# Graph network on one core: the one-hot matrices of the edge layers and convolutions made by ScalarE as 1 minus distance instead of compared by VectorE

## What is computed

```python
h = relu(layernorm(x)); x = x + attention(h, src, dst, ...)       # scores, then a weighted sum by dst
h = relu(layernorm(x))
ea = silu(edge_attr @ We + be)
for l in range(4):                                                 # four edge layers
    agg = segment_sum(relu(h[src] + ea), dst)
    h = layernorm(h + mlp(h + agg)) * gamma + beta
x = x + h
h = relu(layernorm(x)); x = x + conv2(conv1(h))                    # two convolutions: segment_sum(h[src] * norm, dst)
h = relu(layernorm(x)); x = x + segment_sum(h[src] @ W, dst) + h @ W_self
```

## Time and profile before

| | |
|---|---|
| device time, median of three runs | 11198.52 us |
| the profiled execution's own time | 11231.99 us |
| its span, first to last instruction | 11230.1 us |
| busy: PE, VectorE, ScalarE, POOL | 6020.5, 3251.3, 1365.6, 6472.3 us |
| mean granted TensorE clock | 0.723 of full speed |
| scores (POOL's gathers) | about 230 to 1525 us of the span |
| weighted sum | 1692 to 2181 us |
| four edge layers | 2215 to 7519 us |
| three convolutions | 7519 to 11230 us |

### The profile page before, as it was taken

The page is one execution under the profiler, slowest core; times in us unless marked ns, Lnnn a source line. Parts: engine busy times, 40 slices in busy tenths (PEclk is TensorE's granted clock), DMA queues, the critical chain, the costliest instruction groups (busy, mean ns, idle before and its releaser), DMA issues. The chain is left out here.

```text
span 11230.1 us, 158248 instructions
## 1 busy us (share of the span) xinstructions
PE 6020.5 (54%) x23911; PEld 4066.9 (36%) x23912; DVE 3251.3 (29%) x7438; ACT 1365.6 (12%) x2091; POOL 6472.3 (58%) x6737
## 2 busy tenths in 40 slices
PE   2556646566665666756666566653344333433344
PEld 1334425433443333433344333332333233333334
DVE  2334467612232122311223122331122112221222
ACT  1112210011221112211122111210000000000000
POOL 2556526466655665556554655546666566656665
PEclk9566669877887788877888778875666555665566
DMA  4777754233322333323332322221111111111111
GB/s 112 206 208 218 219 152 129 86 85 83 84 80 73 86 82 80 82 74 86 82 80 75 83 80 79 77 57 44 46 47 47 44 44 46 44 42 44 45 46 44
DMA packets 982683, 960.66 MB, mean 86 GB/s; under 512 B 442720, under 2 KB 710395, under 8 KB 982137
## 3 DMA queue, kind: packets, MB, share of 16 engines
q0 software_dynamic: 213248, 462.82, 15.6%
q1 hardware_dynamic: 647644, 399.74, 13.3%
q10 hardware_dynamic: 121756, 97.77, 2.7%
HBM read 801.39 MB, written 164.71 MB: 86 GB/s over the span
## 5 line engine op out<-in xcount | busy, mean ns | idle before, releaser
L700 POOL DMA_INDIRECT rows<-node_rows,idx x5488 | 5386.0, 981 | 3647.5 <-SPq L550 1992.6
L1327 DVE SCALAR_TENSOR_TENSOR onehots<-iota_f,win_base,dst_ch 128x512 f32<-128x512 f32 x1969 | 1567.8, 796 | 6664.0 <-remote 3954.8
L832 PE MATMUL ps_seg<-rows,onehots 128*128 x7840 | 1584.2, 368 | 2422.8 <-DVE sums L1348 1089.9
L832 PEld LDWEIGHTS ps_seg<-rows,onehots 128*128 128x128 f32 x7840 | 1383.6, 265 | 2621.6 <-issue 2617.4
L832 PEld LDWEIGHTS ps_seg<-onehots 128*128 128x128 f32 x7840 | 1178.7, 220 | 1744.6 <-issue 962.5
L832 PE MATMUL ps_seg<-onehots 128*128 128x128 f32 x7840 | 1231.4, 307 | 1066.6 <-DVE sums L1348 466.6
L906 PE MATMUL ps_big<-q_res,ident 128*128 (+1 forms) x1968 | 1277.0, 736 | 766.1 <-issue 325.5
L906 PE MATMUL ps_big<-rows,ident 128*128 (+1 forms) x1968 | 1180.7, 686 | 2.1 <-issue 2.1
L700 POOL DMA_INDIRECT sums<-kv_rows,idx x784 | 775.2, 989 | 528.5 <-SPq L550 302.6
L1051 ACT ACTIVATE onehots<-ps_big 128x512 f32<-128x512 f32 x980 | 576.1, 597 | 3251.0 <-remote 1470.5
L906 PEld LDWEIGHTS ps_big<-rows,ident 128*128 128x128 f32 x1968 | 445.1, 227 | 616.3 <-issue 614.0
(11 more groups left out here) (193 smaller groups left out, 2243.4 us busy)
## 6 DMA issues: line engine op xcount, KB each, us to landing
q_res<-gates_by_edge SPq DMA_DIRECT2D x784, 256.0 KB
rows<-node_rows,idx POOLq DMA_INDIRECT x5488
gates_by_edge<-gate ACTq DMA_DIRECT2D x244, 256.0 KB
rows<-dst_padded SPq DMA_DIRECT2D x196, 256.0 KB
value_rows_by_edge<-sums SPq DMA_DIRECT2D x196, 256.0 KB
rows<-value_rows_by_edge SPq DMA_DIRECT2D x196, 256.0 KB, 3.1
idx<-src_padded SPq DMA_DIRECT2D x1568, 2.0 KB
node_rows<-h_res ACTq DMA_DIRECT2D x49, 448.0 KB
```

What stands on the lines that cost most here:

```text
L700: pool.indirect_dma_start(target[:, r, j, :], None, table, bass.IndirectOffsetOnAxis(ap=idx[:, r, j:j + 1], axis=0)).then_inc(rows_landed[ ...
L832: last = nc.tensor.matmul(ps_seg[u % 2][:, 0:width], onehots[:, u, j, :], rhs(j), start=j == 0, stop=j == J - 1)
L1327: V.scalar_tensor_tensor(onehots[:, u, :, :], iota_f[:, :].rearrange("p (a n) -> p a n", a=1).to_broadcast([P, J, P]), win_base[:, ds(w, 1 ...
```

## The change

ScalarE makes the one-hot matrices of the edge layers and convolutions, as max(0, 1 - |node - target|), in six instructions per step: the four offsets of an edge per partition (window's first node minus target, 128x4, function Identity), then for each column the absolute value of `iota_f` plus that offset (128x128, function Abs, the offset as bias), then Relu of 1 minus all four (128x512). It waits for its own result twice in between. VectorE keeps only the additions there; in the weighted sum it still compares. Since ScalarE now goes through the steps of a convolution, its copies and stores of a group hang behind steps of the next iteration, as they did in the edge layers, and the store of a group comes one group later.

```diff
+            def mark_edges(k, s, u, c, w, buffers):
+                n = sum_no(k) * N_ONEHOT - N_ONEHOT
+                nc.scalar.activation(apart[:, u, :], dst_ch[:, ds(c * J, J)], ACT.Identity, bias=win_base[:, ds(w, 1)],
+                                     scale=-1.0).then_inc(apart_ready, 1)
+                wait_alone(act, "act", apart_ready, n + s + 1)
+                for j in range(J):
+                    last = nc.scalar.activation(onehots[:, u, j, :], iota_f[:, :], ACT.Abs, bias=apart[:, u, j:j + 1])
+                last.then_inc(distance_ready, 1)
+                wait_alone(act, "act", distance_ready, n + s + 1)
+                nc.scalar.activation(onehots[:, u, :, :], onehots[:, u, :, :], ACT.Relu, bias=1.0, scale=-1.0)\
+                    .then_inc(onehot_ready, 1)
+
+            def begin_pass(k):
+                wait_alone(act, "act", segsum_ready, sum_no(k) * N_STEP)
+                mark_edges(k, 0, 0, 0, 0, 2)
+
+            def mark_next(k, s, u, row):
+                wait_alone(act, "act", segsum_ready, sum_no(k) * N_STEP + s)
+                mark_edges(k, s + 1, 1 - u, row.get(CHUNK_, CHUNKS - 1, 1), row.get(WIN_, WINDOWS, 1), 2)
...
             with act.Fori(0, LAYERS) as l:
+                begin_pass(l + L1_PASS)
...
                     nc.scalar.activation(msg[:, u, :, 0:D], ps_big[u][:, :].rearrange("p (j d) -> p j d", d=D), ACT.Relu)\
                         .then_inc(msg_ready, 1)
+                    mark_next(l + L1_PASS, s, u, row)
...
-                with engine_loop(act, 0, GROUPS - 1) as g:
-                    copy_group(sum_no(k), g, copies)
-                    store(g)
+                begin_pass(k)
+
+                def convolve(s, u, turn, row):
+                    mark_next(k, s, u, row)
+
+                def conv_store(g):
+                    with act.If(g != 0):
+                        store(one_before(g, GROUPS))
+                each_step(act, "act", convolve, behind={2: lambda g: copy_group(sum_no(k), g, copies), 3: conv_store})
                 copy_group(sum_no(k), GROUPS - 1, copies)
+                store(GROUPS - 2)
                 store(GROUPS - 1)
...
             def add_previous(k, s, u, row, width):
 
+                wait_alone(dve, "dve", segsum_ready, sum_no(k) * N_STEP + s)
                 dve.wait_ge(agg_added, s - 1 + sum_no(k) * N_AGG)
...
                 def edge_layer(s, u, turn, row):
-                    mark_next(k, s, u, row)
                     if not is_first(s):
                         add_previous(k, s, u, row, D)
...
                 def convolve(s, u, turn, row):
-                    mark_next(k, s, u, row)
                     if not is_first(s):
                         add_previous(k, s, u, row, D)
```

More of the change, by code:

```diff
@@ L124, in build_program @@
         part = sb("part", [P, FH])
+        apart = sb("apart", [P, 2, J])
         attr_t = sb("attr_t", [P, 2, P])
@@ L286, in build_program @@
         msg_ready = sem("msg_ready")
+        apart_ready = sem("apart_ready")
+        distance_ready = sem("distance_ready")
         node_in_ready = sem("node_in_ready")
@@ L1336, in begin_pass @@
                     wait_alone(dve, "dve", agg_cleared, sum_no(k) * GROUPS)
-                mark_edges(k, 0, 0, 0, 0)
-            def mark_next(k, s, u, row):
-                dve.wait_ge(segsum_ready, sum_no(k) * N_STEP + s)
-                mark_edges(k, s + 1, 1 - u, row.get(CHUNK_, CHUNKS - 1, 1), row.get(WIN_, WINDOWS, 1))
             def add_previous(k, s, u, row, width):
+                wait_alone(dve, "dve", segsum_ready, sum_no(k) * N_STEP + s)
                 dve.wait_ge(agg_added, s - 1 + sum_no(k) * N_AGG)
@@ L1435, in _ @@
             begin_pass(1)
+            mark_edges(1, 0, 0, 0, 0)
             def mark_ahead(s, u, row, n):
@@ L1446, in attend @@
                 if not is_first(s):
-                    dve.wait_ge(segsum_ready, s)
                     add_previous(1, s, u, row, AGGW)
```

## The result

The changed kernel takes 11532.07 us (median of 4 runs, 11519.61 to 11569.58) against 11203.8 us of the kernel before in the same session (4 runs, 11189.39 to 11227.47): ratio 1.0286, 95% interval 1.0267 to 1.0305. It is 2.9% slower. The forecast was 11390 us with a range of 11060 to 11660.

A forecast was written before the change was run, and what follows sets the result against it. The prediction took POOL's gathers, plus holes where POOL waits for a free slot, as the bound. Gathers -90, convolutions +210 and edge layers +70 gave +190 us on 11198.5, rounded to 11390 us, range 11060 to 11660.

The forecast's parts named there:

- Relief of the gathers, -90 us: POOL's gathers, no longer stretched by compares running beside them, give back half of at most 187 us: -90 us.
- The mark 1.6 us later: ScalarE's six instructions take 2.3 us against 0.75 us of the compare, so the one-hot matrix comes 1.6 us later.
- Convolutions, 70 us each: The later matrix after POOL's holes costs 70 us per convolution, 210 us for three; upper end 585 us.
- One delay per hole: In convolutions, each POOL hole is charged one late mark: 49 holes per 1227 us, 49 x 1.6 = 78 us.
- Edge layers, 17 us each: ScalarE's slower loop costs a fifth of 1.0 us at each of 84 holes: 17 us per layer, 70 for four.
- The prediction's loop of ScalarE: In edge layers, ScalarE's own work takes 3.6 us per step, 1.0 us over TensorE's burst.
- the chain from one sum to the next matrix: In edge layers, the new chain needs 3.5 us and fits in the 4.2 us available.
- Moved work: Convolution copies and clears ahead of marks, 42 us of ScalarE's time, taken as hidden; the later store, 3 us, within rounding.
- the signs of being right: Gathers' mean 960 to 970 ns; POOL's convolution waits about 190 us per 1000; an edge layer within 30 us of 1280.
- The sign against it: A convolution under 1227 us would show the forecast wrong and speak for Rival B.
- Rival A: ScalarE becomes the bound, an edge layer costing 1334 us: +510 us in all, 11710 us; chance 0.17.
- Rival B: Holes end when POOL stops, the later matrix falls into ring slack, POOL keeps 187 us: 11050 us; chance 0.24.

The follow-up runs named there:

- e7: The kernel before with every one-hot compare of the edge layers and convolutions left out, matrices keeping old contents: 9080.56 us, ratio 0.9822.
- e8: The kernel before with VectorE making each matrix in four 128x128 compares with one SBUF tensor each, not one 128x512 with two: 9117.12 us, ratio 0.9865.
- e6: The changed kernel, unchanged, run again in a session where the kernel before took 9243 us: 9234.16 us, ratio 0.999.
- e12: The changed kernel with ScalarE's marks of the edge layers made two steps ahead: 11406.31 us, ratio 1.0185 to the kernel before.
- e2: The change in the convolutions alone, with VectorE comparing again in the edge layers: 9209.17 us, ratio 0.9959 to the kernel before.
- e5: The kernel before, unchanged, traced in a faster session: 9244.58 us, ratio 0.9998.
- e9: The kernel before with two of the four gathers per chunk in edge layers and convolutions: 7738.6 us.
- e10: The changed kernel with two of the four gathers per chunk in edge layers and convolutions: 8490.87 us.

## Why the prediction was right, and where it was not

The direction stands and 11532 us lies in the range: the later matrix costs where the gathers don't set the pace, and that outweighs the gathers' relief. But the split of the sum was wrong, and one error took back part of another: without the 78 us by which the relief was set too low, the forecast would have been 11310 us, further off. That 11390 came as near as it did owes something to this luck.

- **Relief of the gathers, -90 us.** Measured 5386.0 - 5217.6 = 168 us, of the 187 that were there to be had. I took half because "a part of the stretched ones may be due to other work". The step that failed is that halving: e7 gives 166.5 us without any compare, e8 152 us with compares of another form, so nearly the whole excess was the compare's, as the 165 us of gathers that start beside one say too. The Trainium skill's rule that the prediction weighed beside it (SBUF — State Buffer, "Who interferes with whom") had it right.
- **The mark 1.6 us later.** Right: 2.44 us against 0.75, the 128x128 ones 389 ns where the bounds were 357 and 493. The compare is dearer in the sum than it was, though: its mean of 796 ns had the weighted sum's in it, those removed took 754.
- **Convolutions, 70 us each.** Measured 28, 50 and 23 net. POOL's busy time fell by 33, 28 and 26 us in them, so the charge was 63 on average gross. One delay per hole was a fair count on the 11.2 ms chip. On a 9.2 ms chip, with no holes there, a convolution of e6 is shorter by what POOL's busy time fell (15, 20 and 14 us against 16, 19 and 15): the charge is zero, which bears out that it is the holes that are charged. That it is the mark's delay there and not the lower clock (0.60 to 0.54) isn't shown.
- **Edge layers, 17 us each.** This term failed. Measured 47 net, and with the 21 us by which POOL's busy time fell, 68 gross. The prediction's loop of ScalarE, 3.6 us per step, was near (3.39 in the drain of e6, 0.8 over TensorE's 2.61); "I take a fifth of the 1.0 us" per hole was not, and had no row behind it. Two things stood in its place. The prediction let the chain from one sum to the next matrix fit (3.5 us in 4.2), so nothing was charged for it; e12, which takes that wait away, gets 122 us back, 30 per layer. And with a queue of steps to go through, every step goes at ScalarE's pace, not a fifth of one, as the drains show: that is in the 150 us that e12 leaves. The drain at the end of a layer, 38 us against 28 (33 against 11 on a 9.2 ms chip), is 10 of the 68 us; how the rest lies over the bursts, no run separates.
- **Moved work.** Taken as hidden. The 8 us outside the passes leave no room for much of it there; its share within the convolutions no run separates.
- **Sum.** Gross 4 x 68 + 3 x 63 + 7 (weighted sum) + 8 = 476, less POOL's relief of 171 by stages (168 by the page): 305 us, against 280 - 90 = 190 forecast.
- **The signs.** Of the signs of being right three failed: the gather's mean is 951 ns, not 960 to 970, POOL's wait in the edge layers rose from 203.3 to 248.1 us per 1000, and the first edge layer is 48 us longer, not within 30. POOL's wait in the convolutions rose from 138.6 to 165.7, not to 190. The sign against it, a convolution under 1227 us, is not met by the 1217 above: taken as the prediction took it, from the end of the pass before, the first is 1254 us long (7721 to 8975).

Rival A (ScalarE becomes the bound) holds in part: its sign, "edge layers longer by more than convolutions", is there, 47 against 34, but ScalarE is busy for 760 of 1329 us, and the time is well under 11710. It is the bound in the bursts and the drains of the edge layers, not of a layer as a whole. Rival B's gain of the gathers came whole, yet its condition (holes as many and as long as before) did not hold: POOL's waits for a slot grew by 394 us. On the 9.2 ms chips POOL has none in the convolutions, and there they do gain: e2, -37 us. The prediction charged its costs by the hole, so without holes it would have said -90 us or more; measured were -9 (e6). What it lacked for that case is the drain and the fourth edge layer, where ScalarE's pace costs as much as the gathers give.

What the holes are is still open, and wasn't settled by the runs: nothing in the program differs between e5 and the kernel before.

## What to carry to other kernels

Before work is moved to another engine to free a shared resource, try the same work on the same engine in a form that doesn't touch the resource: four tensor_scalar compares kept nearly all the relief (-126 us where the move gave -9), and cost 195 us where the gathers were halved against the move's 752. A chain that is hidden behind a pacing engine has a price all the same, to be read by making the pacing engine's work smaller; where that engine stalls for reasons of its own, a part of this price comes due. And when a mean is to be split into causes, look at each instruction with what ran when it started: the 829 gathers that start beside a compare stood in the trace before the forecast was made, and give 165 of the 189 us where half was assumed.

## What was not expected of the hardware

Two of four sessions ran the same program in 17% less time, 9244 us against 11204, each steady within about 0.4%. Among the rows that differ are SyncE's semaphore instructions. Line 550 in the kernel before on the 11.2 ms chip, and in e5, the same program on a 9.2 ms chip (ns, min/median/max):

```profile
L550 SPq EVENT_SEMAPHORE  x1568: 2/17/1405, 230.9 to 11196.1; - x196
...
L550 SPq EVENT_SEMAPHORE  x1568: 17/17/17, 233.0 to 9196.2; - x196
```

In e5 each takes 17 ns, in the first trace up to 1405 ns at the same median: some instructions are held up there, and signals of TensorE seem to reach the others late (the waits that the earlier trace rows put down to `remote`, the compare of the earlier trace rows). In e5 that releaser is gone: the same compares wait 4833.3 us for `PE ps_seg`, as the program says. What holds them up, no run here shows. That VectorE's waits for a releaser unknown to the profile are 3954.8 us with all gathers and 691.5 with half of them (e9), in the change 3889.0 and 337.2 (e10), suggests that it goes with POOL's gathers. e8 wasn't run on an 11.2 ms chip with all gathers; its gain there is open.
